# Attention and product-key experts on one core: score steps among the experts' outputs, eight one-hot rows beside the roots, q and k scaled before the pairs, norm rows moved to steps 24 and 25

## What is computed

```
q, k, v = heads of x @ w_qkv.T            # 16 heads of width 8
q, k    = rope(rms_norm(q) * w), rope(rms_norm(k) * w)
x       = layernorm(x + softmax(causal(q @ k.T * scale)) @ v @ w_proj.T)
xn      = rms_norm(x) * norm_w
sim1,sim2 = xn @ w_q.T, each with its 32 keys     # 8 heads, two sides
s, i    = top_k(sim, 8) on each side              # 8 values of 32
fs, pk  = top_k(s1[:, None] + s2[None, :], 8)     # 8 pairs of 64
fi      = the expert's number of each pair, of 1024
hidden  = gelu(xn . expert_down[fi]) * relu(fs)
x       = layernorm(x + sum of hidden * expert_up[fi])
```

## Time and profile before

| what | us |
|---|---|
| median of 3 runs | 1625.49 (1624.69 to 1626.4) |
| profiled execution, its own time | 1626.17 |
| span of the profiled execution | 1624.4 |
| busy: PE, DVE | 1353.0, 1358.7 |
| busy: ACT, POOL | 926.0, 665.0 |
| mean granted TensorE clock | 0.904 |

### The profile page before, as it was taken

How to read it: one execution, slowest core, us unless ns; L and a number is a source line. 1 busy time by engine, 2 the same in 40 slices (tenths; PEclk the granted TensorE clock), 3 DMA queues, 4 the chain that set the end, 5 groups by cost and what they waited for, 6 DMA issues and landing times.

```text
span 1624.4 us, 55167 instructions
## 1 busy us (share of the span) xinstructions
PE 1353.0 (83%) x21008; PEld 973.5 (60%) x21008; DVE 1358.7 (84%) x6568; ACT 926.0 (57%) x1502; POOL 665.0 (41%) x1024
## 2 busy tenths in 40 slices
PE   3567788989898998989898998989898988977567
PEld 3333456657575766667574766666575756655557
DVE  3314599999999898999999998999999998798984
ACT  0665766666675666666666766666666756442110
POOL 1412627171725436171826345270817355050410
PEclk9977899989898999989898999989898999998676
DMA  3000000000000000000000000000000000000000
GB/s 85 7 1 14 1 8 9 8 16 9 16 9 15 3 15 9 8 15 9 15 9 15 9 15 2 9 16 8 16 8 16 3 15 3 2 15 2 9 1 17
DMA packets 29989, 18.81 MB, mean 12 GB/s; under 512 B 1824, under 2 KB 29216, under 8 KB 29728
## 3 DMA queue, kind: packets, MB, share of 16 engines
q1 hardware_dynamic: 29728, 15.23, 3.3%
HBM read 11.04 MB, written 4.19 MB: 9 GB/s over the span
## 4 chain that ended last, share of the span: by engine, by line
PE 41%; DVE 36%; ACT 9%; issue 8%; POOL 5%; SPq 1%; DVEq 0%; DMA 0%; ACTq 0%; POOLq 0%
DVE onehot L1263 10%; PE G L938 7%; PE OV L827 7%; PE F L883 7%; DVE topi L1209 6%; PE G L927 6%; DVE psel L1225 4%; DVE whot L1288 3%; PE S L813 3%; DVE topv L1203 3%; ACT prob L631 3%; DVE fsel L1220 2%; DVE hid L1301 2%; PE S L753 2%; PE F L893 2%
## 5 line engine op out<-in xcount | busy, mean ns | idle before, releaser
L631 ACT ACTIVATE prob<-S 128x512 f32<-128x512 f32 x640 | 371.0, 596 | 146.7 <-PE S L815 140.4
L927 PE MATMUL G<-whot,onehot 128*128 128x16 bf16 x12288 | 383.5, 170 | 33.4 <-DVE hid L1301 19.6
L927 PEld LDWEIGHTS G<-whot,onehot 128*128 128x128 bf16 x12288 | 364.8, 97 | 68.2 <-issue 18.4
L1263 DVE TENSOR_TENSOR onehot<-lo_no,elo 128x1024 bf16<-128x1024 uint16 x512 | 386.4, 806 | 0.0
L827 PE MATMUL OV<-prob,vp 128*9 128x512 f32 (+3 forms) x2048 | 183.6, 508 | 67.9 <-ACT prob L631 62.0
L494 POOL TENSOR_TENSOR gat<-gat,cande 128x1280 f16<-128x1280 f16 x64 | 178.6, 2790 | 75.9 <-DVE gat L1231 75.9
L815 PE MATMUL S<-causal,ident_b 128*128 128x128 bf16 x1024 | 200.9, 229 | 0.0
L813 PE MATMUL S<-qT,kT_even 128*128 128x512 bf16 (+3 forms) x512 | 145.1, 312 | 53.7 <-ACT prob L631 45.0
L503 POOL COPY y<-y_new 128x512 f32<-128x512 f32 x16 | 9.8, 611 | 434.2 <-DVE r L1187 376.7
L563 ACT ACTIVATE hid<-F 128x512 f32<-128x512 f32 x128 | 76.6, 598 | 188.3 <-PE F L883 188.3
L827 PEld LDWEIGHTS OV<-prob,vp 128*9 128x9 f32 x2048 | 54.9, 99 | 198.2 <-issue 107.2
(11 more groups left out here) (134 smaller groups left out, 2498.7 us busy)
## 6 DMA issues: line engine op xcount, KB each, us to landing
xa<-in_L_attn_x SPq DMA_DIRECT2D x16, 256.0 KB, 2.9
xr<-in_L_attn_x SPq DMA_DIRECT2D x16, 256.0 KB, 3.0
out<-r SPq DMA_DIRECT2D x16, 256.0 KB, 2.3
onehot<-in_L_ffn_expert_down SPq DMA_DIRECT2D x1, 512.0 KB, 6.0
up<-in_L_ffn_expert_up SPq DMA_DIRECT2D x1, 512.0 KB, 6.6
onehot<-in_L_ffn_keys SPq DMA_DIRECT2D x1, 256.0 KB, 6.4
onehot<-in_L_attn_w_qkv SPq DMA_DIRECT2D x1, 192.0 KB, 4.4
onehot<-in_L_attn_w_proj SPq DMA_DIRECT2D x1, 64.0 KB, 4.7
```

The costliest lines, as they stand in the source:

```text
L631: act.activation(dst, src, ACT.Exp, scale=SCALE).then_inc(exp_done.sem, 1)
L927: last = nc.tensor.matmul(bank[:, 16 * i:16 * i + 16], onehot[:, row, :], whot[:, t, w_part, :], start=(w_part == 0), stop=(w_part == 2))
L1263: return dve.tensor_tensor(onehot[:, row:row + 8, :].rearrange("p t (c i) -> p t c i", i=2), lo, e, ALU.is_equal)
```

## The change

Nothing that is computed changes; the order does, on three engines.

- TensorE: the four tiles of expert outputs stand at steps 4, 5, 6 and 7, with the scores of steps 5 to 7 between them, and `project_out` behind the second. The hidden products move from step 4 to step 8; behind them stand weight parts 0 to 2, `transpose_yi`, part 3 and the first similarities. Parts 4 to 31 keep their steps 9 to 38. The third group of `transpose_stack` moves from step 35 to 33, the last `turn_numbers` and `transpose_selection` from 35 to 36.
- ScalarE: Gelu, `normed` and the first similarities move to step 8, the rows of norm 1 to step 24, those of norm 2 to 25, and the copies of the third group of q and k to 33.
- VectorE: one-hot rows 16 to 23, not 16 to 19, stand between the steps of the roots; quarter 1 of the weighted one-hots moves from ahead of norm 1 to behind the shifts, ahead of weights 0; half 1 of q and k is scaled ahead of the first `top_pairs`; the last `top_pairs` stands ahead of weights 5.

```diff
--- before.py
+++ after.py
@@ -282,7 +282,7 @@
 
 
         S_ORDER = [("scores", n) for n in range(NG * UNITS)]
-        QK_STEPS = [27, 31, 35, 39]
+        QK_STEPS = [27, 31, 33, 39]
         for g in reversed(range(NG)):
             at = S_ORDER.index(("scores", QK_STEPS[g])) + 1
             S_ORDER[at:at] = [("Q", g), ("K", g)]
@@ -345,10 +345,10 @@
 
 
 
-        SIMS_STEPS = [8, 9, 13, 15]
-        NUMBER_STEPS = [22, 28, 34, 35]
-        SELECTION_STEP = 35
-        WEIGHT_STEPS = [n for n in range(5, 39) if n not in (19, 29)]
+        SIMS_STEPS = [9, 13, 15]
+        NUMBER_STEPS = [22, 28, 34, 36]
+        SELECTION_STEP = 36
+        WEIGHT_STEPS = [n for n in range(9, 39) if n not in (19, 29)]
 
         block = ctx.enter_context(nc.Block())
 
@@ -670,18 +670,20 @@
                             taken_qk(nxt, 1)
                         if late is not None:
                             taken_outputs(late)
-                    if n == 4 and older is not None:
-                        for c in range(NHI):
-                            hidden(older, c)
-                    if n == 7 and late is not None:
-                        normed(late)
-                    if late is not None and n in (8, 9):
-                        similarities(late, n - 8)
+                    if n == 8:
+                        if older is not None:
+                            for c in range(NHI):
+                                hidden(older, c)
+                        if late is not None:
+                            normed(late)
+                            similarities(late, 0)
+                    if n == 9 and late is not None:
+                        similarities(late, 1)
                     if nxt is not None and n in (13, 17):
                         first_parts(nxt, (n - 13) // 4)
-                    if n == 12 and late is not None:
+                    if n == 24 and late is not None:
                         norm1_rows(late)
-                    if n == 13 and oldest is not None:
+                    if n == 25 and oldest is not None:
                         norm2_rows(oldest)
                     if nxt is not None and n in (20, 21):
                         second_parts(nxt, n - 20)
@@ -961,25 +963,29 @@
                             project_qk(nxt, 1, b)
                         if late is not None:
                             turn_outputs(late)
-                    if step == 4:
-                        if oldest is not None:
-                            expert_outputs(oldest, range(2))
-                        if late is not None:
-                            project_out(late)
-                        if oldest is not None:
-                            expert_outputs(oldest, range(2, NT))
+                    if 4 <= step < 8 and oldest is not None:
+                        expert_outputs(oldest, [step - 4])
+                    if step == 5 and late is not None:
+                        project_out(late)
+                    if step == 8:
                         if older is not None:
                             hidden_products(older)
+                            for part in range(3):
+                                weights(older, part)
+                        if late is not None:
+                            transpose_yi(late)
+                        if older is not None:
+                            weights(older, 3)
+                        if late is not None:
+                            project_similarities(late, 0)
                     if nxt is not None and step in QK_STEPS:
                         transpose_stack(nxt, QK_STEPS.index(step), b)
                     if older is not None and step in WEIGHT_STEPS:
-                        weights(older, WEIGHT_STEPS.index(step))
-                    if step == 7 and late is not None:
-                        transpose_yi(late)
+                        weights(older, 4 + WEIGHT_STEPS.index(step))
                     if b is not None and u == 1 and g:
                         transpose_o(b, g - 1)
                     if late is not None and step in SIMS_STEPS:
-                        project_similarities(late, SIMS_STEPS.index(step))
+                        project_similarities(late, SIMS_STEPS.index(step) + 1)
                     if late is not None and step in NUMBER_STEPS:
                         turn_numbers(late, NUMBER_STEPS.index(step))
                     if late is not None and step == SELECTION_STEP:
@@ -1314,8 +1320,6 @@
                 if nxt is not None:
                     squares_summed(nxt)
                 one_hots(hot(14, 16))
-                if older is not None:
-                    weighted_one_hots(older, 1)
                 if late is not None:
                     norm1_moments(late)
                 if oldest is not None:
@@ -1327,17 +1331,16 @@
                 first = AT_QK if nxt is not None else AT_NORM1 if late is not None else AT_NORM2
                 last = AT_NORM2 if oldest is not None else AT_NORM1 if late is not None else AT_QK
                 if nxt is not None or late is not None or oldest is not None:
-                    roots(turn, slice(first.start, last.stop), hot(16, 20))
+                    roots(turn, slice(first.start, last.stop), hot(16, 24))
                 else:
-                    one_hots(hot(16, 20))
+                    one_hots(hot(16, 24))
                 if late is not None:
                     norm1(late)
                 if oldest is not None:
                     norm2_shift(oldest)
-                one_hots(hot(20, 23))
                 if older is not None:
+                    weighted_one_hots(older, 1)
                     apply_weights(older, 0)
-                one_hots(hot(23, 24))
                 if late is not None:
                     top_keys(late, 0)
                     top_keys(late, 1)
@@ -1349,10 +1352,10 @@
                     normalise_o(b, 0)
                 if older is not None:
                     weighted_one_hots(older, 2)
-                if late is not None:
-                    top_pairs(late, 0)
                 if nxt is not None:
                     normalise(nxt, 1)
+                if late is not None:
+                    top_pairs(late, 0)
                 if older is not None:
                     apply_weights(older, 2)
                 if late is not None:
@@ -1371,10 +1374,10 @@
                     apply_weights(older, 4)
                 if late is not None:
                     top_pairs(late, 2)
+                if late is not None:
+                    top_pairs(late, 3)
                 if older is not None:
                     apply_weights(older, 5)
-                if late is not None:
-                    top_pairs(late, 3)
                 if b is not None:
                     normalise_o(b, 2)
                 if older is not None:
```

More of the change, by code:

```diff
@@ L1351, in iteration @@
                     weighted_one_hots(older, 2)
+                if nxt is not None:
+                    normalise(nxt, 1)
                 if late is not None:
                     top_pairs(late, 0)
-                if nxt is not None:
-                    normalise(nxt, 1)
                 if older is not None:
```

## The result

The changed kernel takes 1660.87 us (median of 4 runs, 1659.04 to 1667.21) where the one before takes 1625.79 (median of 4): a ratio of 1.0223, 95% interval 1.0195 to 1.0251. It is slower by 35 us; 1628 was forecast, and 1640 was the upper end of the range.

A forecast was written before the change was run, and what follows sets the result against it. VectorE was taken to bound the kernel (busy 83.76 of a 90.31 us turn). Four terms sum to +0.21 us a turn, 2.5 us over twelve turns, giving 1628 us; range 1611 to 1640.

The forecast's parts named there:

- Part 1: Decode to norm 2: with step 36 and part 29 moved out, norm 2 starts earlier; -0.97 us a turn.
- Part 2: Norm 2 to first top keys: four more one-hots and the moved quarter (3.27 us) come in; +1.66 us a turn.
- the second rival: VectorE and GpSimd alternate in the moved quarter, which takes 4.3 us; a turn +1.2 us, total 1640 us; chance 0.07.
- Part 3: Top keys to last one-hots: the whole wait ahead of weights 3 goes; -1.42 us a turn.
- Part 4: Last one-hots to decode: step 36's scores and part 29 lengthen the wait for the selection; +0.94 us a turn.
- The third rival: TensorE reaches part 28 late, with a low clock through steps 20 to 25; about 1.1 us a turn, 1641 us; chance 0.10.
- the one-hots escape GpSimd: One-hots 24 to 27 avoid the slowdown from GpSimd's third parts; 1.7 us a turn saved, total 1607.5 us; chance 0.25.
- They alternate: In the moved quarter VectorE and GpSimd take turns: 4.3 us, a turn +1.2 us, total 1640 us; chance 0.07.
- late at part 28: TensorE comes late to part 28, about 1.1 us a turn on top of the 0.21; total 1641 us; chance 0.10.

The follow-up runs named there:

- the first experiment: The changed kernel with quarter 1 of the weighted one-hots ahead of norm 1 again: 1657.06 us, ratio 1.0193.
- the best version: Kernel before with norm rows at 24 and 25, half 1 scaled first, last pairs ahead of weights 5: 1615.2 us, then 1618.45 us.

## Why the prediction was wrong

The measured pieces come close to the whole: eight one-hots and quarter +20.5 (1643.78 - 1623.25), selection +12.1, outputs and step 8 +6.0, norm rows with scaling and pairs 3 -5.9, q and k at 33 none: +32.7, where the change costs 35.1. They do not add in general: the outputs cost 6.0 alone and 11.2 in the change, and the norm rows alone gain 5 when put back into it.

**Part 1 failed** in the sentence that TensorE runs 22.22 us "nearly without a stop" and that step 36 and part 29 "leave this stretch, minus 0.94". TensorE did leave them behind, but 13.1 us behind decode it needs o from VectorE, which works without a stop until then: before, it came 0.4 behind the start of o. The stretch has two parallel paths up to there, and the forecast shortened one. Missed: 1.26 us a turn, some 15 of the 35; 0.94 of it is this, the rest that the output tiles with their score steps took 1.09 more and not 0.93, and that norm 2 starts 0.38 behind step 8 and not 0.20. Two pairs of runs show it: with the outputs spread, norm 2 stands 23.48 behind decode with the selection at 36 and 23.49 at 35; with the outputs at step 4, 22.39 at both. The selection ahead of decode gives this stretch nothing.

**Part 2 was right in kind, and a term was too small.** The roots cost 1.8, for 1.7 in the forecast. The quarter cost 4.02, not 3.27, and what decides was named in the second rival, at 3.4 us and above; it was given 0.07. The rule of the Trainium skill cited there (SBUF — State Buffer, "SBUF: two separate sides") fits this stretch: four of GpSimd's instructions slipped in. The three one-hots of 1.89 in the earlier trace rows, on which I relied, went the other way; why, no run here settles. Missed: 0.82, some 10 us. But a right price for the quarter would not have been enough. Without it in that place, as the first experiment shows, the top keys start 14.4 behind norm 2 at full clock and up to 15.8 at the lower one, 15.2 in the mean, where 14.75 was forecast: sims bind. The lower clock at the similarities, in eight turns of twelve, was not in the forecast at all.

**Part 3 was right in size, for another reason in part.** The wait ahead of weights 3 went. But with the top keys 2.5 later, and half 1 scaled earlier, it goes with the norm rows in their old place too. Top_pairs 3 ahead of weights 5 was not "nothing": it gives the late chunk time, and without it the wait moves there.

**Part 4 was right in its 0.94** and too small by 0.61. TensorE reached part 28 without waiting, 0.8 behind weights 6. What failed is "about 2 us late at step 27, as much as it is ahead": that is so only while the clock stays at 1.00, as in the next turn, where the wait is the forecast 2.80. In two turns of three the clock falls behind the wait at step 27, and then 0.6 or 1.5 us come on top, 0.6 in the mean of the twelve turns. The sum had nothing for this. The third rival named it, but at steps 20 to 25.

**Of the rivals,** "the one-hots escape GpSimd" was false (4.43 where 4.26 stood), and it held a quarter of the chance. "They alternate" and "late at part 28" were both true at once, and I had priced them one at a time; but together they are 1.4 a turn. The largest single error, Part 1, was in no rival. What stays open: why the clock falls behind a wait in one turn and not behind the same wait in the next, and what the norm rows at 24 and 25 cost outside the full turns (5 us in the changed kernel).

## What to carry to other kernels

When work is moved across a point at which another engine waits, one wait grows for sure; the other side shrinks only if the moving engine is the longer of the two paths to the next meeting. So look up at each meeting, even one that shows no wait, how long the operand had been ready. Here o was taken 0.44 us behind its start, as soon as it is taken after a wait (0.43), which means that both engines bind. An instruction put into a dependent chain costs its own time only while its engine has other work for the round trip that the chain starts; four one-hots of 0.43 cost 1.9 us a turn, of a delay of 2.29, 0.95 of which was the lower clock behind the new wait. One turn can mislead where turns differ: look at several before reading a wait or a clock as the kernel's. And of eight edits that came together, three that gain 6 us were hidden under four that lose 39 when timed apart from them.

## What was not expected of the hardware

Behind short waits of TensorE its granted clock often fell, and not always. Behind waits of 0.95 and 1.18 us for yi, and behind one of 1.63 for one-hots, it went to the level of 1.2 GHz for a few us; behind the first two, a pair of products of 128x512 took 2.04 and 2.05 instead of 1.10. In the changed kernel the wait for yi is 0.94 to 0.96 in every turn, and the pair behind it takes 1.96 to 2.05 in eight turns and 1.10 in four; the wait of 1.5 at step 27 is followed by 0.72 in one turn and by 1.00 in the next. So a wait on a path that ends in a wait of VectorE may cost nearly double, or nothing. In the best version the same kernel runs its turns in 88.75 or in 90.5 us, as the clock stays down for a shorter or longer time behind the norm rows.

VectorE's weighted one-hots and GpSimd's rotation alternated one for one (3.38 for three that take 1.90 at rest; 1.16 to 1.17 for each of GpSimd's), in the changed kernel and, within 0.01, with the two one-hot edits alone.
